# Four-bit feed-forward stage: VectorE's turn begins elsewhere, h goes over in two transfers, down is cut in two

## What is computed

```python
def fp4_quant_dequant(x):          # blocks of 16 along the last axis
    scale = max(max|x| / 6, 1e-12)
    idx = searchsorted(_MID, |x / scale|)
    return _GRID[idx] * sign(x / scale) * scale
gate, y = fp4_linear(x, w_gate), fp4_linear(x, w_up)     # 512 -> 1408
h = silu(gate) * y
x = x + tanh(g_ffn[1]) * fp4_linear(h, w_down)           # 1408 -> 512
```

## Time and profile before

| | |
|---|---|
| median of three runs | 2104.51 us (2102.99 to 2106.59) |
| profiled execution | 2105.52 us |
| its span in the profile | 2103.7 us |
| TensorE / VectorE / GpSimd / ScalarE busy, whole span | 87% / 68% / 59% / 47% |
| the four-bit stage | from about 1760 us to the end |
| granted TensorE clock, whole span | 0.94 of full speed |

### The profile page before, as it was taken

How to read it: one execution, slowest core, us unless ns; L and a number is a source line. 1 busy time by engine, 2 the same in 40 slices (tenths; PEclk the granted TensorE clock), 3 DMA queues, 4 the chain that set the end, 5 groups by cost and what they waited for, 6 DMA issues and landing times. The chain is left out here.

```text
span 2103.7 us, 41058 instructions
## 1 busy us (share of the span) xinstructions
PE 1840.1 (87%) x14583; PEld 1278.3 (61%) x14610; DVE 1431.5 (68%) x2597; ACT 994.1 (47%) x1276; POOL 1243.0 (59%) x1465
## 2 busy tenths in 40 slices
PE   5799999999998459997578999999999977899995
PEld 3467777777776348876346666667667663344442
DVE  4667767867765368886344767768677645899862
ACT  3167767766767497775214434434434341111110
POOL 3267767767766435434212667777677435989962
PEclk9799999999997579999889999999999988999997
DMA  7435445445430321111533444544445553234232
GB/s 207 105 105 130 119 113 130 123 119 131 114 101 25 116 96 36 52 44 35 181 103 88 119 125 134 149 128 136 141 130 148 123 112 78 68 70 93 72 73 56
DMA packets 271258, 222.41 MB, mean 106 GB/s; under 512 B 150008, under 2 KB 239864, under 8 KB 270584
## 3 DMA queue, kind: packets, MB, share of 16 engines
q1 hardware_dynamic: 271096, 220.22, 39.0%
HBM read 129.96 MB, written 67.53 MB: 94 GB/s over the span
## 5 line engine op out<-in xcount | busy, mean ns | idle before, releaser
L739 POOL TENSOR_TENSOR a_p_hl<-a_p,a_p_hl 125x448 bf16<-125x448 f32 x540 | 568.8, 1055 | 437.2 <-ACT a_p_hl L910 408.6
L900 ACT ACTIVATE a_p<-a_psum 125x1344 f32<-125x1344 f32 x192 | 247.8, 1291 | 142.7 <-PE a_psum L1353 132.4
L1084 DVE TENSOR_REDUCE a_nm<-a_psum 112x1 f32<-112x750 f32 x256 | 237.3, 933 | 100.9 <-PE a_psum L1373 100.2
L910 ACT ACTIVATE a_p_hl<-a_p 125x1344 bf16<-125x1344 f32 x192 | 253.9, 1323 | 85.7 <-PE a_psum L1391 82.0
L1391 PEld LDWEIGHTS a_psum<-a_v_st,a_p_hl 125*128 125x128 bf16 x4608 | 177.6, 98 | 46.0 <-issue 26.7
L1391 PE MATMUL a_psum<-a_v_st,a_p_hl 125*128 125x65 bf16 (+2 forms) x4608 | 189.2, 195 | 16.6 <-issue 5.8
L1263 PE MATMUL a_psum<-a_chl,a_w 128*128 128x375 bf16 x768 | 144.0, 334 | 21.5 <-DVE a_w L974 14.7
L1263 PE MATMUL a_psum<-a_chl,kept_w 128*128 128x375 bf16 x768 | 134.7, 327 | 20.6 <-DVE kept_w L974 17.8
L1373 PE MATMUL a_psum<-a_k_st,a_q_st 96*112 96x375 bf16 x512 | 130.8, 342 | 21.7 <-DVE a_nm L1084 15.8
L1263 PE MATMUL a_psum<-a_w,a_chl 128*125 128x512 bf16 x576 | 140.7, 387 | 8.3 <-DVE a_m_parts L1065 5.7
L875 ACT ACTIVATE a_v_st<-a_psum 125x512 bf16<-125x512 f32 x96 | 58.2, 607 | 188.8 <-PE a_psum L1263 188.8
(11 more groups left out here) (263 smaller groups left out, 3892.1 us busy)
## 6 DMA issues: line engine op xcount, KB each, us to landing
a_k<-a_k_tmp SPq DMA_DIRECT2D x64, 375.0 KB, 3.0
a_k_st<-a_k SPq DMA_DIRECT2D x96, 187.5 KB, 3.4
kept_k<-a_k SPq DMA_DIRECT2D x96, 187.5 KB, 3.4
a_c<-in_ctx_t SPq DMA_DIRECT2D x16, 750.0 KB, 5.8
ctx_parts<-a_chl SPq DMA_DIRECT2D x16, 750.0 KB, 9.1
a_chl<-ctx_parts SPq DMA_DIRECT2D x16, 750.0 KB, 6.1
a_q_st<-a_q SPq DMA_DIRECT2D x192, 56.0 KB, 2.2
parts<-a_fhl SPq DMA_DIRECT2D x24, 352.0 KB, 3.7
```

The costliest lines, as they stand in the source:

```text
L739: ins = nc.gpsimd.tensor_tensor(p_hl[0:MC, h % 2, 1, cols], p32[0:MC, h % 2, cols], p_hl[0:MC, h % 2, 0, cols], ALU.subtract)
L900: nc.scalar.activation(p32[0:MC, par, :].rearrange("p (b n) -> p b n", b=3), st[0:MC, :, 0:2 * S], ACT.Exp, scale=scale).then_inc(exp_done, 1)
L910: nc.scalar.activation(p_hl[0:MC, par, 0, :], p32[0:MC, par, :], ACT.Copy).then_inc(phi_done, 1)
L1084: ins = nc.vector.tensor_reduce(out, sm_[0:HALF, 0:2, 0:MK], AX.XY, ALU.max, negate=True)
```

## The change

Four things. VectorE's turn(t) begins with the three `make_h(t+1, g)` and their x work; the moments, `h_divide(t+1)`, `h_powers` and `h_lo(t)` follow, and y(t-1) is last; the first moments, division and powers are written out ahead of turn 0, and its loop covers two turns fewer. SyncE's `turn_hidden(t)` now stands in turn t behind the loads and ahead of the output store, and sends h's high half after `hhi_ready` and `down_ready`, and the low half after `hb_ready`. ScalarE's `h_hi` waits for the high transfer, VectorE's `h_lo` for the low one. TensorE computes down's 22 terms with h's high part between the second and the third column group, and the 11 with its low part behind the third; it waits for each half where it needs it.

```diff
--- before.py
+++ after.py
@@ -2267,7 +2267,7 @@
         moments, roots = sem("moments"), sem("roots")
         xn_ready, x_scaled, xq_ready = sem("xn_ready"), sem("x_scaled"), sem("xq_ready")
         xhi_ready, xb_ready, xT_in = sem("xhi_ready"), sem("xb_ready"), sem("xT_in")
-        hhi_ready, hb_ready, hT_in = sem("hhi_ready"), sem("hb_ready"), sem("hT_in")
+        hhi_ready, hb_ready, hiT_in, loT_in = sem("hhi_ready"), sem("hb_ready"), sem("hiT_in"), sem("loT_in")
         gu_ready, th_ready, h_made = sem("gu_ready"), sem("th_ready"), sem("h_made")
         h_scaled, hq_ready = sem("h_scaled"), sem("hq_ready")
         down_ready, y_ready = sem("down_ready"), sem("y_ready")
@@ -2314,16 +2314,19 @@
 
             def turn_hidden(t):
 
+                sp.wait_ge(hhi_ready, t + 1)
+                sp.sem_inc(sp_steps, 1)
+                if not (number_known(t) and t == 0):
+
+                    sp.wait_ge(down_ready, t)
+                    sp.sem_inc(sp_steps, 1)
+                sp.dma_start(hqT[:, 0, :, :], hb[:, 0, :], transpose=True).then_inc(hiT_in, 16)
                 sp.wait_ge(hb_ready, t + 2)
                 sp.sem_inc(sp_steps, 1)
-
-                sp.wait_ge(y_ready, t + 1)
-                sp.sem_inc(sp_steps, 1)
-                sp.dma_start(hqT[:, :, :, :].rearrange("p a c s -> p (a c) s"),
-                             hb[:, :, :].rearrange("p a f -> p (a f)"), transpose=True).then_inc(hT_in, 16)
+                sp.dma_start(hqT[:, 1, :, :], hb[:, 1, :], transpose=True).then_inc(loT_in, 16)
 
             sp.sem_inc(out_sent, 1)
-            sp.sem_inc(hT_in, 1)
+            sp.sem_inc(hiT_in, 1)
             for t in (2, 3):
 
                 sp.wait_ge(xn_ready, t)
@@ -2332,8 +2335,6 @@
                     turn_input(t - 1, (t - 1) % 2)
 
             def turn(t, par):
-                if in_range(t - 1):
-                    turn_hidden(t - 1)
                 if in_range(t + 2):
                     turn_input(t + 2, par)
                 if in_range(t - 1):
@@ -2348,6 +2349,8 @@
                     sp.sem_inc(sp_steps, 1)
                     sp.dma_start(xin[:, :], x_in[bass.ds(t + 4, 1), :, :].rearrange(
                         "o p d -> p (o d)")).then_inc(x_in_s, 16)
+                if in_range(t):
+                    turn_hidden(t)
                 if in_range(t - 1):
 
                     sp.wait_ge(y_ready, t + 1)
@@ -2450,7 +2453,7 @@
                 act.wait_ge(hq_ready, t + 1)
                 if not (number_known(t) and t == 0):
 
-                    act.wait_ge(hT_in, t * 16 + 1)
+                    act.wait_ge(hiT_in, t * 16 + 1)
                 nc.scalar.activation(hb[:, 0, :], hq[:, :], ACT.Copy).then_inc(hhi_ready, 1)
 
             def turn(t, par):
@@ -2517,16 +2520,12 @@
 
             def h_lo(t, par):
                 dve.wait_ge(hhi_ready, t + 1)
+                if not (number_known(t) and t == 0):
+
+                    dve.wait_ge(loT_in, t * 16)
                 nc.vector.tensor_tensor(hb[:, 1, :], hq[:, :], hb[:, 0, :], ALU.subtract).then_inc(hb_ready, 1)
 
             def turn(t, par):
-                if in_range(t + 3):
-                    x_moments(t + 3)
-                if in_range(t):
-                    h_divide(t, par)
-                    h_powers()
-                if in_range(t - 1):
-                    h_lo(t - 1, 1 - par)
                 for g in range(NG):
                     if in_range(t + 1):
                         make_h(t + 1, 1 - par, g)
@@ -2536,6 +2535,13 @@
                         x_normalise(t + 3)
                     if g == 1 and in_range(t + 3):
                         x_scale(t + 3)
+                if in_range(t + 4):
+                    x_moments(t + 4)
+                if in_range(t + 1):
+                    h_divide(t + 1, 1 - par)
+                    h_powers()
+                if in_range(t):
+                    h_lo(t, par)
                 if in_range(t - 1):
                     dve.wait_ge(xres_in, t * 16)
                     dve.wait_ge(down_ready, t)
@@ -2558,8 +2564,17 @@
             make_h(0, 0, 1)
             x_scale(2)
             make_h(0, 0, 2)
-            turns(dve.Fori, turn, lambda i: own.enter_loop(i, 2 * FFN1_LINKS),
-                  lambda: own.leave_loop((T - 4) // 2))
+            x_moments(3)
+            h_divide(0, 0)
+            h_powers()
+            turn(0, 0)
+            with dve.Fori(0, (T - 6) // 2) as i:
+                own.enter_loop(i, 2 * FFN1_LINKS)
+                for n in range(2):
+                    turn(i * 2 + (1 + n), 1 - n)
+            own.leave_loop((T - 6) // 2)
+            for t in range(T - 5, T + 1):
+                turn(t, t % 2)
 
         @block.tensor
         def _(pe):
@@ -2580,17 +2595,24 @@
                 ins.then_inc(gu_ready, 1)
 
             def turn(t, par):
-                for g in range(NG):
+                for g in range(NG - 1):
                     if in_range(t + 1):
                         gate_up(t + 1, 1 - par, g)
                 if in_range(t - 1):
-                    pe.wait_ge(hT_in, t * 16 + 1)
+                    pe.wait_ge(hiT_in, t * 16 + 1)
 
                     pe.wait_ge(y_ready, t)
                     for c in range(FC):
-                        for j, (a, b) in enumerate(SPLIT_TERMS):
-                            ins = nc.tensor.matmul(down[:, :], hqT[:, a, c, :], wd[:, b, c, :],
-                                                   start=(c == 0 and j == 0), stop=(c == FC - 1 and j == 2))
+                        for b in range(2):
+                            nc.tensor.matmul(down[:, :], hqT[:, 0, c, :], wd[:, b, c, :],
+                                             start=(c == 0 and b == 0), stop=False)
+                if in_range(t + 1):
+                    gate_up(t + 1, 1 - par, NG - 1)
+                if in_range(t - 1):
+                    pe.wait_ge(loT_in, t * 16)
+                    for c in range(FC):
+                        ins = nc.tensor.matmul(down[:, :], hqT[:, 1, c, :], wd[:, 0, c, :],
+                                               start=False, stop=(c == FC - 1))
                     ins.then_inc(down_ready, 1)
 
             pe.wait_ge(kept.first_turned, 32)
```

## The result

The changed kernel takes 2082.32 us (median of four runs, 2081.76 to 2085.63); the kernel before, 2103.75 over four. The ratio is 0.9902, 95% interval 0.9882 to 0.9922. The profiled execution took 2082.36 us with a span of 2080.6. That is 20.6 us by the ratio and 21.4 by the medians, where 19.1 were forecast; the forecast median was 2085.4 us, 3.1 above the measured one.

The account below looks back on a forecast made before the run. A loop of waits through VectorE's division, transfer, down and y bounds the kernel; GpSimd's loop is next. Savings of 3.5 by the last gate group, 6.8 and 8.8 make 19.1 us, from 2104.51 to 2085.4, range 2082 to 2089.

Parts of the forecast that it names:

- the rival in which TensorE's loop binds: Four-bit stage loop: TensorE, not GpSimd, sets 21.4 us a turn, 3 us less in all, 2082.2; chance 0.14.
- the forecast's mechanism: Four-bit stage loop: with VectorE's wait for down gone, GpSimd's loop binds at 21.75 us a turn; chance 0.58.
- 21.75 was the sum: GpSimd's turn: 21.64 us from the early turns of before, plus 0.1 because x_lo meets the root's last steps.
- The 4.5 us for y(0): Early turns: TensorE waits 4.5 us for y(0); a slow clock there could add up to 2 us.
- the last 33 matmuls: Last tile's down on TensorE: 9.2 us, between 7.1 at full clock and 9.53 at the clock of before.
- the line through two sizes: Transposing transfers: 1.84 us plus 1.23 per thousand columns, so 3.6 us for a half, bounds 3.1 and 5.3.
- The port rule: VectorE's two-SBUF-input instructions and GpSimd's hold a shared port pair exclusively; the loser blocks for the whole instruction.
- The case for a split of bandwidth: VectorE and GpSimd share bandwidth instead of locking: GpSimd's loop shorter than TensorE's, time 2082.2; chance 0.14 with that case.
- its ring: Loop from y through high matmuls, gate group, make_h, division and h_lo: 20.3 us, under TensorE's 21.3, so not binding.
- the 6.8 us for the last division: End of the stage: 6.8 us gained because the last division no longer stands behind a down and a y.
- The 8.8 us for the last tile's chain: Last tile, from h's rounding done to y's start: 13.3 us in place of 22.1, a gain of 8.8.
- the case of no gain per turn: Loop: waits for y or locks replace the wait for down, turns stay 22.33, 5.2 us more, 2090.6; chance 0.19.

Follow-up runs that it names:

- after: The changed kernel, y moved behind h_lo and transfer and down split, against the kernel before: 2082.32 us, ratio 0.9902.
- split only: The changed kernel with y back ahead of the moments and h_divide; half transfers and split down stay: ratio to the kernel before 0.9894.
- last tile on VectorE: The changed kernel with y(11) ahead of h_lo(12), VectorE rounding the last h, and its own tile for that h transposed: ratio to the kernel before 0.9878.
- root ahead of x_round: The changed kernel with GpSimd's square root of the next x directly behind h_round, x_round after it: ratio to the kernel before 0.9964.

## Why the prediction was right, and where it was not

**The time alone decides little.** 2082.32 us is 3.1 below the forecast and nearer to the rival in which TensorE's loop binds (2082.2). That the forecast's mechanism holds and not that one is read from the trace: turns of 21.76 and not 21.4, with GpSimd waiting for nobody.

**The turn.** 21.75 was the sum and 21.76 is measured. The step that carried it was to look for turns of before in which the wait was already absent, and to find GpSimd's loop of 21.64 there. Nine turns took 195.8 us in both.

**TensorE's and VectorE's margins.** VectorE was to be 0.4 us early at h_divide: it waits 0.53. TensorE was to lose about 0.4 a turn to y: its turns are 21.76 for 21.38 without a wait, so 0.38, of which 0.22 is shown as waiting. That holds from turn 7 on; in turns 2 to 5 it ran 21.38 and caught up. The 4.5 us for y(0) are 4.62.

**The end, counted from h_round(1).** Last gate group done: 246.3 forecast, 246.3 measured (2042.48 + 1.95 less 1798.16). Last division 247.4, 247.6. Last down 270.4 (2072.1 less 1801.72), 270.5. Then the one term that was off: the last 33 matmuls, 9.2 forecast, 8.69 measured (2068.63 to y's start at 2077.32), at a granted clock of 0.85 in that stretch. From y to the end 3.24, 3.28. S is 0.4 less than forecast, and the rest of the difference, about 1 to 2 us, lies in the part of the kernel that the edit doesn't touch and in the scatter of the runs.

**The transfers.** 3.6 forecast from the line through two sizes, 3.5 measured; hidden in the loop, as sending one twice confirms.

**The port rule.** Each engine is delayed by the other, and the root moved beside the reduce shows both directions. The Trainium skill, SBUF — State Buffer, section "SBUF: two separate sides", has the loser blocked for the whole instruction. The traces agree for a single pair: in after, three root operations in a row end at 1837.13, 1838.06 and 1839.60, each just behind one of VectorE's powers and h_lo, which end at 1837.07, 1838.01 and 1839.54. In this sequence one GpSimd operation gets through at each change between two of VectorE's long instructions, and the whole root takes 7.3 us (1834.39 to 1841.67). The case for a split of bandwidth (21.4 a turn) is out.

**What failed is the account of which part pays.** I wrote that y had to leave VectorE's path and that its place behind h_lo has no price because its ring is 20.3 us. It doesn't bind the turn, as I wrote, but that was the wrong question. y(t-1) at its new place ends only after GpSimd's rounding of h(t), the division and h_lo, and so it holds high(t) at 20.4 us behind h_round(t), where the transfer alone would let it start at 16. That is a lag of TensorE in every turn, and not the one wait for y(0) that I noted and priced at up to 2 us for the clock. The last gate group carries it to the end: about 3.6 us at the end, net of the 2.0 that the old place loses there. So of the two parts the split of transfer and down is the whole gain, and more (323.6 to 300.4); y's move gives 12.0 alone and takes 3.6 back once the split is there. Of the credits in my sum, the 6.8 us for the last division need no moved y: with the split and y at its old place the division waits only 2 us, since TensorE's last low terms are short. Counted from the first h_round that division starts at 279.3 us before, 269.2 in after and 265.7 in split only.

**Two slips in the working.** The 8.8 us for the last tile's chain compare 22.1 and 13.3 us that run from the end of ScalarE's copy to y's start, not from the end of the rounding; measured are 12.5. And the case of no gain per turn adds 5.2 us, where its own row puts h_round(10) only 4.1 behind the forecast; the turns of before were 22.20 over the nine that are summed. Neither moves the forecast.

What stays open: how much of the end is the clock. The high terms of the last two downs took 6.2 to 7.9 us after waits of 3.6 to 8.8 us, in no fixed relation to the wait just before (only the last down of the run with the last tile on VectorE, after 1.78 us, ran at full speed). From the last down's start to the end of the span the kernels with a split down took 10.7 to 13.5 us, which blurs S by more than a microsecond. It wasn't tried by itself. And the whole times don't part split only from after; what parts them is where TensorE stands, seen in both pairs of profiles.

## What to carry to other kernels

Before you price a wait that is removed, look for turns at a stage's start or end where it is absent already; they show which loop is next, with its contention. Where one loop paces and another engine has slack, ask also how late in the turn that engine is held, and not only whether its ring is shorter than the turn: a lag of 4.5 us that showed as a wait of 0.2 us a turn came back at the last tile. And the drain of a pipeline is worth its own sum: one tile's chain, moved to an engine that idles there, gave 5.8 us, more than all the loop's turns (4.0).

## What the runs showed of the hardware

- A 128x1 GpSimd operation takes 0.19 us (0.55 for the power, L2387) alone and up to 2.46 us under VectorE's product, powers and h_lo; beside the reduce and the reciprocal (root ahead of x_round, 1873.67 to 1876.4) it stays at 0.19 to 0.22. In the other direction VectorE's 0.89 us powers take 1.98 beside GpSimd's 128x512 passes.
- A transposing transfer from SBUF to SBUF of 128 rows lands after 3.1, 3.5 and 5.3 us for 1024, 1408 and 2816 columns.
- After an idle of 1.8 to 2.4 us TensorE ran 22 matmuls of 512 columns in 4.92 us, at a granted clock of 1.00 (last tile on VectorE, 2066.90 to 2071.80); after 3.6 to 8.8 us of idling in 6.2 to 7.9, at granted clocks of 0.61 to 0.79.
